# Both attentions of a two-layer kernel: value products of four heads at once, ScalarE's other work behind pairs of exponentials, and idle products in three places

## The chip, the cores and the metric

The kernel runs on one core of one Trainium2 chip. A core has TensorE (PE in the rows; PEld is its weight load), VectorE (DVE), ScalarE (ACT), GpSimd (POOL) and SyncE (SP), which issues DMAs. The metric is the device time of the core in microseconds; less is better. SBUF is the working memory, PSUM the matmuls' target, 8 banks of 2 KB per partition.

## The reference

Two layers act on x of 32 batches x 256 tokens x 128 features. Each layer: layer norm with a per-batch scale and shift, attention with 16 heads of 8 features, a residual with a per-batch gain; then layer norm again and a mixture of experts with a second gain.

```python
# layer 0                                     # layer 1
Qn, Kn = Q/|Q|, K/|K|   (per head)            q, kv = x @ Wq, x @ Wkv
attn = softmax(Qn Kn^T / sqrt(8))             attn = softmax(causal(q k^T / sqrt(8)))
out = (attn V) * gates;  x += ga * (out Wo + bo)   x += ga * ((attn V) Wo)
# then 4 experts, token-wise depth            # then top 2 of 8 experts
```

## The kernel before, in words

Every engine has a program written out by hand. Waits on semaphores (s["exp"], s["pv"], s["o"], ...) order them, and each engine runs its own list strictly in that order, so the order of the calls in the loops is the schedule. The phases are: modulation and first layer norm with the start of attention 0, attention 0 (function `dense` of each engine), experts 0, attention 1 (`causal`), rows sent to the experts, experts 1.

Both attentions loop over b = 0..31 (a batch of 256 tokens). A batch has 16 heads, taken two at a time in CH = 8 units u = 0..7. Four heads are a group j = u // 2, and NJ = 4. For each unit:

- TensorE `score(b, u)`: four matmuls (two key tiles x two heads) into the PSUM tile SP[u % 2] (L1873, L2118).
- ScalarE `exp(b, u)`: one exponential of SP[u % 2] into pt[u % 4] in SBUF (L750, L863); from the fifth unit on it waits for s["pv"], the product that frees the buffer.
- Attention 1 only, GpSimd `select(b, u)`: zeroes what the causal mask forbids in pt (L531).
- TensorE `values(b, u)` (L1892, L2138): the values of two heads, fp32, each in 32 columns of the array (tile_position (0, 32g)) and so in 32 partitions of OP. A column of ones beside the values gives the softmax's sum. It is issued two units late. OP has two halves (banks): half 0 holds groups j = 0, 1, half 1 holds j = 2, 3.

VectorE finishes a batch: `tail_t(b, i)` transposes half i of OP in 32 x 32 blocks (L1181, L1343) and raises s["o"]; `tail_n` (in attention 1 `tail_r`, `tail_n`, `tail_a`) divides by the sums and transposes to aT; TensorE's `tail_wo` is the output projection, into the free end of OP's half 1 (L1904, L2150); `tail_w` (L1199, L1366) takes it out and raises s["wr"]; then the gain, the residual `tail_x`, and the statistics of the next layer norm. tail_t(b, 0) closes VectorE's list of batch b, and tail_t(b, 1) stands at the head of the list of b + 1.

Between these, later batches are prepared and earlier ones finished. Attention 0: TensorE `project(b + 3)` (L1859), VectorE `take`, ScalarE `square`, VectorE `lengths` (L1155 and on), GpSimd `lengths` (a Newton iteration), VectorE `unit` (L1165), ScalarE `high` and VectorE `low` (L1174, the fp16 halves), then four transposing DMAs. A finished batch n goes through ScalarE `normal(n)` (needs GpSimd's `deviation`), TensorE `turn(n)` (L1915), ScalarE `enter(n)` (L770), TensorE `router(n)` (L1925), VectorE `extra(n)` (L1229) and `depth(n)`, GpSimd `low(n)`. Attention 1: twelve `fill`s per batch (L2092, L2097, L2101) form scores in M's two banks alternately, so that VectorE's `fill_max` (L1329) finds each row's maximum for the next batch; ScalarE `z2`, `enter`, `raw`, `high`, `z3`, `h3`, `row`; TensorE `enter`, `project` (L2076), `turn3`, `router`, `back`. `keep_warm` issues matmuls whose result nobody reads. From b = 15 on GpSimd also sends rows to the experts' buffers (L492).

## Time and profile before

| what | value |
|---|---|
| median of 3 runs | 1821.77 us (1817.3 to 1825.23) |
| the profiled execution | 1828.18 us, span 1826.0 us |
| TensorE busy | 1556.5 us (85%), 12803 matmuls |
| VectorE busy | 1284.0 us (70%) |
| ScalarE busy | 1188.8 us (65%) |
| GpSimd busy | 882.6 us (48%) |
| mean granted TensorE clock | 0.933 |
| attention 0 | from about 80 to 540 us |
| experts 0 | from about 540 to 770 us |
| attention 1 | from about 800 to 1430 us |
| experts 1 | from about 1500 us on |

The span cut into 40 equal slices of 45.65 us, busy share in tenths (9 is 90% or more), and the granted clock in tenths:

```profile
PE   5799999999967999779999999999999508989970
DVE  6566777777747888836767677675877536777768
ACT  3777788778756989635565665556555517888860
POOL 6254544545511333324444438747465563555554
PEclk9899999999988999969999999999999558999995
```

A row of a timeline gives the start and the time in microseconds, the engine, the line of the kernel, the operation, output and input tiles, their shapes, the count of merged instructions, and in brackets the idle time ahead of it with the engine and line that ended it. A row of a stretch gives its bounds and length, then the busy time and the instructions of TensorE, its weight load, VectorE, ScalarE and GpSimd, the granted TensorE clock as a share of full speed, the DMA engines' busy share and GB/s. Matmuls overlap, so the distance between two starts tells more than a row's length.

### The profile page before, as it was taken

The numbers are of one execution on the slowest core, as the hardware profiler recorded it, in microseconds if no ns is written. First come the engines' busy times: TensorE is split into PE (matmuls) and PEld (weight loads), VectorE is DVE, ScalarE is ACT, GpSimd is POOL, SyncE is SP. The second block draws the span as 40 slices with busy tenths as digits, with TensorE's granted clock in tenths as the row PEclk, the third lists the DMA queues.
The fourth block names the chain that finished last, engine by engine and source line by source line (L and its number), as shares of the span: only waits on it lengthen the run. The fifth ranks groups of instructions, "written<-read, shape, count | busy, mean of one in ns | idle before, by whom it ended". The sixth has DMA issues, their size and how long they took to land.

```text
span 1826.0 us, 39932 instructions
## 1 busy us (share of the span) xinstructions
PE 1556.5 (85%) x12803; PEld 796.7 (44%) x12803; DVE 1284.0 (70%) x3451; ACT 1188.8 (65%) x2134; POOL 882.6 (48%) x1677
## 2 busy tenths in 40 slices
PE   5799999999967999779999999999999508989970
PEld 3334444444433444324444444444444306777750
DVE  6566777777747888836767677675877536777768
ACT  3777788778756989635565665556555517888860
POOL 6254544545511333324444438747465563555554
PEclk9899999999988999969999999999999558999995
DMA  5221112221208930022211213312221323222228
GB/s 155 75 45 36 36 36 41 42 37 36 47 13 331 386 125 1 23 57 50 48 41 41 46 38 66 69 43 66 45 62 43 112 77 97 75 77 76 76 66 258
DMA packets 238478, 141.20 MB, mean 77 GB/s; under 512 B 184163, under 2 KB 210659, under 8 KB 237253
## 3 DMA queue, kind: packets, MB, share of 16 engines
q1 hardware_dynamic: 227072, 119.72, 24.4%
q0 software_dynamic: 8640, 17.97, 3.0%
q8 instruction: 108, 1.77, 0.4%
q10 hardware_dynamic: 2564, 0.97, 0.2%
q14 instruction: 94, 0.76, 0.1%
HBM read 37.67 MB, written 58.98 MB: 53 GB/s over the span
## 4 chain that ended last, share of the span: by engine, by line
PE 42%; DVE 12%; issue 6%; ACT 2%; DVEq 2%; POOL 2%; DMA 1%; POOLq 1%; SPq 0%; ACTq 0%; another core or an unknown queue 0%
PE OP L2138 8%; PE OP L2003 5%; PE M L2101 5%; PE SP L1983 4%; DVE mx L1329 4%; PE SP L2298 3%; PE SP L2118 2%; PE M L2076 2%; PE M L2097 2%; PE M L2092 2%; PE OP L2313 2%; DVE pt L1620 2%; POOL h_dram L492 1%; PE OP L2150 1%; PE M L1993 1%
## 5 line engine op out<-in xcount | busy, mean ns | idle before, releaser
L863 ACT ACTIVATE pt<-SP 128x768 f32<-128x768 f32 x256 | 207.1, 809 | 250.4 <-PE SP L2118 236.4
L1329 DVE TENSOR_REDUCE mx<-M 128x2 f32<-128x512 f32 (+1 forms) x384 | 258.0, 683 | 104.5 <-PE M L2101 94.6
L531 POOL TENSOR_SCALAR_AFFINE_SELECT pt<-pt 128x256 f32<-128x256 f32 x512 | 198.6, 412 | 262.8 <-ACT pt L863 260.9
L750 ACT ACTIVATE pt<-SP 128x1024 f32<-128x1024 f32 x256 | 255.2, 1019 | 72.1 <-PE SP L1873 72.0
L562 POOL DMA_INDIRECT y_dram<-hT,dest x142 | 140.2, 987 | 134.2 <-DVE hT L1626 112.0
L964 ACT ACTIVATE pt<-SP,b 128x256 f16<-128x256 f32 x284 | 138.2, 487 | 81.8 <-PE SP L2298 81.2
L1892 PE MATMUL OP<-pt,vs 128*32 128x256 f32 x1408 | 186.5, 387 | 0.0
L492 POOL DMA_INDIRECT h_dram<-hT,slot x128 | 130.7, 1021 | 58.8 <-issue 31.7
L2138 PE MATMUL OP<-pt,vs 128*32 128x128 f32 (+1 forms) x1408 | 151.0, 338 | 4.7 <-POOL pt L531 4.7
L1620 DVE TENSOR_TENSOR pt<-vs,pt 128x256 f16<-128x256 f32 x284 | 115.7, 428 | 49.8 <-ACT vs L965 25.0
L656 POOL TENSOR_TENSOR st<-st,ksT 128x512 f32<-128x512 f32 x48 | 72.0, 1500 | 153.1 <-DVE ksT L1751 153.0
L965 ACT ACTIVATE vs<-SP,b 128x256 f32<-128x256 f32 x284 | 139.5, 491 | 0.0
L2298 PE MATMUL SP<-ksT,shared 128*128 128x256 f16 x852 | 129.6, 276 | 10.0 <-DVE ksT L1595 10.0
L2313 PE MATMUL OP<-shared,pt 128*128 x1704 | 130.6, 219 | 0.4 <-issue 0.2
L1734 DVE TENSOR_TENSOR pt<-vs,pt 128x512 f16<-128x512 f32 x128 | 104.7, 830 | 26.6 <-ACT vs L982 25.2
L577 POOL TENSOR_TENSOR nt<-rn 128x64 f32<-128x64 f32 x96 | 34.2, 357 | 166.3 <-DVE rn L1018 156.7
L2313 PEld LDWEIGHTS OP<-shared,pt 128*128 128x128 f16 x1704 | 107.1, 98 | 12.5 <-issue 0.8
L980 ACT ACTIVATE pt<-SP,b 128x512 f16<-128x512 f32 x128 | 88.0, 688 | 26.5 <-PE SP L1983 23.0
L2101 PE MATMUL M<-ksT,shared 24*128 24x128 f16 (+1 forms) x704 | 105.2, 250 | 0.0
L1873 PE MATMUL SP<-shared 32*128 32x256 f16 x1024 | 100.3, 274 | 3.6 <-ACT pt L750 3.5
L1892 PEld LDWEIGHTS OP<-pt,vs 128*32 128x32 f32 x1408 | 66.6, 109 | 72.0 <-ACT pt L750 19.6
L2138 PEld LDWEIGHTS OP<-pt,vs 128*32 128x32 f32 x1408 | 67.0, 110 | 69.5 <-issue 22.7
(325 smaller groups left out, 3344.9 us busy)
## 6 DMA issues: line engine op xcount, KB each, us to landing
h_dram<-shared SPq DMA_DIRECT2D x8, 4488.0 KB, 33.5
hT<-h_dram SPq DMA_DIRECT2D x71, 132.0 KB
rows<-g_dram SPq DMA_DIRECT2D x4, 2048.0 KB, 7.1
pt<-y_dram SPq DMA_DIRECT2D x32, 256.0 KB, 3.7
x_sb<-in_x SPq DMA_DIRECT2D x8, 512.0 KB, 8.8
pt<-in_w SPq DMA_DIRECT2D x4, 1024.0 KB
out<-x_sb SPq DMA_DIRECT2D x16, 256.0 KB, 3.0
shared<-st SPq DMA_TRANSPOSE x144, 2.4
```

Of the source, the lines that this page charges most:

```text
L492: pool.indirect_dma_start(out=h_dram, out_offset=bass.IndirectOffsetOnAxis(ap=slot[:, TT * b0 + t, k:k + 1], axis=0), in_=hrow[:, q % 2, t ...
L531: last = pool.affine_select(out=diag, in_=diag, compare_op=ALU.is_ge, fill=0.0, base=0, pattern=[[0, 2], [1, P]], channel_multiplier=-1)
L562: pool.indirect_dma_start(out=y_dram, out_offset=bass.IndirectOffsetOnAxis(ap=dest[:, g % XB, r:r + 1], axis=0), in_=ys[:, g % XB, r, :], ...
L750: act.activation(pt[:, u % 4], SP[u % 2][:], ACT.Exp, scale=SCALE).then_inc(s["exp"], 1)
L863: act.activation(pt[:, u % 4, :, 0:384], SP[u % 2][:, :, 0:384], ACT.Exp, scale=SCALE).then_inc(s["exp"], 1)
L1329: dve.tensor_reduce(to, M[:, k % 2, :].rearrange("p (j k) -> p j k", j=4 if k < 4 else 2), AX.X, ALU.max).then_inc(s["mred"], 1)
L1620: dve.tensor_tensor(hid1[:, g % 2, f, 1, :], relu[:, f, 0:BLK], hid1[:, g % 2, f, 0, :], ALU.subtract).then_inc(k["lo"], 1)
L1892: last = pe.matmul(OP[32 * g:32 * g + 32, j // 2, c:c + T], vsd[b % 3][:, k, HG * j + g, :], pt[:, u % 4, i, k * T:k * T + T], start=(k == ...
L2101: last = pe.matmul(v[:, n, :], qs3[b % 3][32 * g:32 * g + 3 * DH, j, q0:q0 + P], ks3[b % 3][32 * g:32 * g + 3 * DH, j, 0:kn], start=False, ...
L2138: last = pe.matmul(OP[32 * g:32 * g + 32, j // 2, c + q0:c + T], vs3[b % 3][:, k, HG * j + g, :], pt[:, u % 4, i, k * T:k * T + T - q0], s ...
L2298: last = pe.matmul(bank[f][:, 0:BLK], w16[1][:, 0, u, bass.ds(e * (F1 * P) + f * P, P)], hg[:, g % 2, v, :], start=(n == 0), stop=(n == 2))
L2313: last = pe.matmul(to[:, r, :], hid1[:, g % 2, f, v, r * P:(r + 1) * P], w16[1][:, 1, u, bass.ds(e * (F1 * P) + f * P, P)], start=False, s ...
```

## The change

- `values(b, j)` replaces `values(b, u)`: four heads (16 matmul records) in one go, interleaved over the four column groups, at every odd u, when both exponentials (in attention 1 both selects) are there. It raises s["pv"] by 2. At u = 1 it is group 3 of the batch before.
- ScalarE in attention 0: `normal`, `high`, `square` and `enter` stand behind pairs of exponentials; `normal` and `enter` handle batch b - 4, not b - 3.
- TensorE in attention 0: the two halves of `project` are at u = 2 and u = 4 (before both at u = 1), `turn(b - 4)` at u = 6, `router(b - 5)` at u = 2 of the next batch. GpSimd's `low`, VectorE's `extra` and `depth` handle b - 5. `extra` moves behind `tail_n`.
- Idle products: attention 0, four after score(b, 0) into OP's half 0, which wait for s["o"] >= 2b - 1 (tail_t(b - 1, 0)), and three after the turn at u = 6 into half 1, which wait for s["wr"] >= b. Attention 1, one before the third, fifth and sixth fill, where no `keep_warm` stands.
- Attention 1: the product comes before the fills of u = 1 and after the first fill of u = 3; TensorE's `enter(b + 3)` is behind score 7 and ahead of the product, `turn3(b - 5)` behind the product of u = 7. On VectorE the tail steps come one to three column maxima earlier.

```diff
@@ ScalarE, dense
     for b in range(B):
         exp(b, 0)
         exp(b, 1)
+        if b >= 4:
+            normal(b - 4)
         exp(b, 2)
         if b == 0:
             sigmoid()
+        exp(b, 3)
         if b + 2 < B:
             high(b + 2)
-        exp(b, 3)
         exp(b, 4)
+        exp(b, 5)
         if b + 3 < B:
             square(b + 3)
-        if b >= 3:
-            normal(b - 3)
-        exp(b, 5)
         exp(b, 6)
-        if b >= 3:
-            enter(b - 3)
         exp(b, 7)
+        if b >= 4:
+            enter(b - 4)
         if b < CHUNKS:
             weight_high(0, b)
-    for n in range(B - 3, B):
+    for n in range(B - 4, B):
         normal(n)
         enter(n)
...
@@ VectorE, dense
     static_gate()
     dve.drain()
     for b in range(B):
-        if b >= 4:
-            extra(b - 4)
         if b == 1:
             dve.wait_ge(gate_in, 16 * HG)
             dve.wait_ge(row_in, 16)
         if b:
             tail_t(b - 1, 1)
             tail_n(b - 1)
+        if b >= 5:
+            extra(b - 5)
         if b + 2 < B:
             unit(b + 2)
         if b + 3 < B:
...
@@ VectorE, causal
                 fill_max(b + 1, k)
                 if k in (7, 11):
                     max_row(b + 1, k // 11)
+            if b and k == 0:
+                tail_t(b - 1, 1)
             if b and k == 2:
-                tail_t(b - 1, 1)
-            if b and k == 4:
                 tail_r(b - 1)
-            if b and k in (5, 6):
-                tail_n(b - 1, k - 5)
-            if b and k == 7:
+            if b and k in (3, 4):
+                tail_n(b - 1, k - 3)
+            if b and k == 5:
                 tail_a(b - 1)
             if b and k == 10:
                 tail_w(b - 1)
...
@@ TensorE, dense: values
                                  start=True, stop=True, tile_position=(r0, 0))
         last.then_inc(s["score"], 1)
-    def values(b, u):
-        if u == 0:
+    def values(b, j):
+        if j == 0:
             pe.wait_ge(s["vs"], b + 1)
-        pe.wait_ge(s["exp"], CH * b + u + 1)
-        if b and u % 4 == 0:
-            pe.wait_ge(s["o"], 2 * b + u // 4 - 1)
-            if u:
+        pe.wait_ge(s["exp"], CH * b + 2 * j + 2)
+        if b and j % 2 == 0:
+            pe.wait_ge(s["o"], 2 * b + j // 2 - 1)
+            if j:
                 pe.wait_ge(s["wr"], b)
-        j = u // 2
+        c = (j % 2) * T
         for k in range(TT):
-            for i in range(2):
-                g = 2 * (u % 2) + i
-                c = (j % 2) * T
+            for g in range(HG):
                 last = pe.matmul(OP[32 * g:32 * g + 32, j // 2, c:c + T],
                                  vsd[b % 3][:, k, HG * j + g, :],
-                                 pt[:, u % 4, i, k * T:k * T + T],
+                                 pt[:, 2 * (j % 2) + g // 2, g % 2, k * T:k * T + T],
                                  start=(k == 0), stop=(k == TT - 1),
                                  skip_group_check=True, tile_position=(0, 32 * g))
-        last.then_inc(s["pv"], 1)
+        last.then_inc(s["pv"], 2)
     def tail_wo(b):
...
@@ TensorE, dense: idle
             last = pe.matmul(M[:, 1, t * nx:(t + 1) * nx], hcur[:, n % 2, t * P:(t + 1) * P], wx[1][:],
                              start=True, stop=True)
         last.then_inc(s["lg"], 1)
+    def idle(half, n):
+        for _ in range(n):
+            pe.matmul(OP[:, half, :].rearrange("p (n q) -> p n q", n=4), identb[:],
+                      maskQ[:].unsqueeze(1).to_broadcast([P, 4, P]), start=True, stop=True, skip_group_check=True)
     for n in range(B + 2):
         gates(n)
...
@@ TensorE, dense: the loop
             score(b, u)
             if b == 0 and u == 2:
                 pe.wait_ge(gl_in, 1)
-            if CH * b + u >= 2:
-                values((CH * b + u - 2) // CH, (u - 2) % CH)
-            if u == 1 and b + 3 < B:
-                for t in range(TT):
-                    project(b + 3, t)
+            if u % 2 and CH * b + u >= 3:
+                values((CH * b + u - 3) // CH, (u - 3) % CH // 2)
+            if u == 0 and b:
+                pe.wait_ge(s["o"], 2 * b - 1)
+                idle(0, 4)
+            if u == 2 and b >= 5:
+                router(b - 5)
+            if u in (2, 4) and b + 3 < B:
+                project(b + 3, u // 2 - 1)
             if u == 4 and b:
                 tail_wo(b - 1)
-            if u == 5 and b >= 3:
-                turn(b - 3)
-            if u == 7 and b >= 3:
-                router(b - 3)
-    values(B - 1, CH - 2)
-    values(B - 1, CH - 1)
+            if u == 6 and b >= 4:
+                turn(b - 4)
+                pe.wait_ge(s["wr"], b)
+                idle(1, 3)
+    values(B - 1, NJ - 1)
     tail_wo(B - 1)
-    for n in range(B - 3, B):
+    router(B - 5)
+    for n in range(B - 4, B):
         turn(n)
         router(n)
...
@@ TensorE, causal: the loop (values there is as above, with s["sel"])
         done = 0
         for u in range(CH):
             score(b, u)
-            if FILLS[u] and b + 1 < B:
-                fill(b + 1, done)
-                done += 1
-            if CH * b + u >= 2:
-                values((CH * b + u - 2) // CH, (u - 2) % CH)
             if u == 0 and b + 2 < B:
                 project(b + 2, 0)
                 project(b + 2, 1)
             if u == 4 and b:
                 tail_wo(b - 1)
-            for _ in range(FILLS[u] - 1):
-                if b + 1 < B:
+            if u == 7 and b + 3 < B:
+                enter(b + 3)
+            for n in range(max(FILLS[u], 1)):
+                if n == (u == 3) and u % 2 and CH * b + u >= 3:
+                    values((CH * b + u - 3) // CH, (u - 3) % CH // 2)
+                if FILLS[u] and b + 1 < B:
                     if done == 2 and b in WARM:
                         keep_warm(b, u + 1, WARM[b])
+                    elif done in (2, 4, 5) and b:
+                        pe.wait_ge(s["o"], 2 * b - 1)
+                        idle(0, 1)
                     fill(b + 1, done)
                     done += 1
             if u == 5 and b >= 6:
                 router(b - 6)
                 back(b - 6)
-            if u == 6:
-                if b + 3 < B:
-                    enter(b + 3)
-                if b >= 5:
-                    turn3(b - 5)
+            if u == 7 and b >= 5:
+                turn3(b - 5)
             if u == 7 and b - 1 in CHOSEN:
                 positions(CHOSEN.index(b - 1))
-    values(B - 1, CH - 2)
-    values(B - 1, CH - 1)
+    values(B - 1, NJ - 1)
     tail_wo(B - 1)
     for n in range(B - 5, B + 1):
         if n < B:
```

## Rows read from the trace of the kernel before

**Rows 1.** busy time and granted clock: first attention, second attention, after a stand

```profile
172.00:514.00 342.00, 333.12 (x2710) 142.53 (x2708) 247.20 (x734) 271.32 (x370) 164.15 (x484) 1.00 0.20 38
898.00:1070.00 172.00, 164.22 (x1436) 80.01 (x1434) 122.98 (x293) 103.88 (x178) 72.41 (x172) 1.00 0.22 43
131.40:135.00 3.60, 3.60 (x20) 1.00 (x16) 0.97 (x3) 3.35 (x5) 2.36 (x8) 0.53 0.49 99
```

**Rows 2.** timeline, ScalarE: last exponentials of batches 0, 8, 28, 31

```profile
90.25 1.95 ACT L750 ACTIVATE pt<-SP 128x1024 f32<-128x1024 f32 x2
...
208.06 1.03 ACT L750 ACTIVATE pt<-SP 128x1024 f32<-128x1024 f32 x1
...
486.28 1.03 ACT L750 ACTIVATE pt<-SP 128x1024 f32<-128x1024 f32 x1
...
524.50 1.03 ACT L750 ACTIVATE pt<-SP 128x1024 f32<-128x1024 f32 x1
```

**Rows 3.** timeline, TensorE, one batch of the first attention

```profile
305.71 0.66 PE L1925 MATMUL M<-wx,hcur 128*128 128x68 f32 x4
306.30 0.39 PE L1873 MATMUL SP<-shared 32*128 32x256 f16 x4
...
307.94 1.06 PE L1892 MATMUL OP<-pt,vs 128*32 128x256 f32 x8
308.92 1.56 PE L1859 MATMUL M<-wqkv,hT 128*128 128x384 f32 x4
310.41 0.39 PE L1873 MATMUL SP<-shared 32*128 32x256 f16 x4
...
314.34 0.71 PE L1904 MATMUL OP<-wo,aT 128*128 128x128 f32 x4
```

**Rows 4.** timeline, TensorE, two products in a row

```profile
525.45 1.18 PE L1892 MATMUL OP<-pt,vs 128*32 128x256 f32 x16
```

**Rows 5.** timeline, VectorE, two batches of the first attention

```profile
307.36 0.70 DVE L1181 STREAM_TRANSPOSE oT<-OP 128x512 f32<-128x512 f32 x1
...
309.04 0.72 DVE L1181 STREAM_TRANSPOSE oT<-OP 128x512 f32<-128x512 f32 x1 [0.80 <-PE OP L1892]
...
312.23 1.01 DVE L1147 TENSOR_TENSOR shared<-M,bqkv 128x384 f32<-128x384 f32 x2
315.09 0.43 DVE L1199 TENSOR_TENSOR ao<-OP,bo 128x256 f32<-128x256 f32 x1 [1.84 <-PE OP L1904]
...
317.15 0.68 DVE L1155 TENSOR_REDUCE n<-sq 128x64 f32<-128x512 f32 x1
...
321.95 0.71 DVE L1181 STREAM_TRANSPOSE oT<-OP 128x512 f32<-128x512 f32 x1
...
329.02 0.42 DVE L1199 TENSOR_TENSOR ao<-OP,bo 128x256 f32<-128x256 f32 x1 [2.09 <-PE OP L1904]
...
331.78 0.68 DVE L1155 TENSOR_REDUCE n<-sq 128x64 f32<-128x512 f32 x1
...
334.81 0.70 DVE L1181 STREAM_TRANSPOSE oT<-OP 128x512 f32<-128x512 f32 x1
```

**Rows 6.** timeline, TensorE, one batch of the second attention

```profile
994.61 1.56 PE L2076 MATMUL M<-wqkv,hT 128*128 128x384 f32 x4
...
999.94 0.84 PE L2138 MATMUL OP<-pt,vs 128*32 128x256 f32 x8
1000.72 0.28 PE L2097 MATMUL M<-maskQ,identb 128*128 128x256 bf16 x1
...
1013.81 1.56 PE L2076 MATMUL M<-wqkv,hT 128*128 128x384 f32 x4
```

**Rows 7.** timeline, ScalarE, end of a batch of the second attention

```profile
1009.94 0.81 ACT L863 ACTIVATE pt<-SP 128x768 f32<-128x768 f32 x1 [1.02 <-PE SP L2118]
...
1012.10 0.81 ACT L863 ACTIVATE pt<-SP 128x768 f32<-128x768 f32 x1 [0.86 <-PE SP L2118]
1012.81 0.56 ACT L833 ACTIVATE hT<-M,modT 128x256 f32<-128x256 f32 x1
```

More of the change, by code:

```diff
@@ L638, in dense @@
                         place_v(b + 2)
-                    if b >= 4:
-                        low(b - 4)
+                    if b >= 5:
+                        low(b - 5)
                     if b + 3 < B:
@@ L644, in dense @@
                         weight_low(b - 1)
-                low(B - 4)
                 deviation(B // 2 - 1)
-                for n in range(B - 3, B):
+                for n in range(B - 5, B):
                     low(n)
@@ L1295, in dense @@
                         tail_x(b - 1)
-                    if b >= 4:
-                        depth(b - 4)
+                    if b >= 5:
+                        depth(b - 5)
                     if b:
@@ L1311, in dense @@
                 variance(B // 2 - 1)
-                for n in range(B - 4, B):
+                for n in range(B - 5, B):
                     extra(n)
@@ L2121, in score, with values @@
                     last.then_inc(s["score"], 1)
-                def values(b, u):
-                    if u == 0:
+                def values(b, j):
+                    if j == 0:
                         pe.wait_ge(s["vs"], b + 1)
-                    pe.wait_ge(s["sel"], CH * b + u + 1)
-                    if b and u % 4 == 0:
-                        pe.wait_ge(s["o"], 2 * b + u // 4 - 1)
-                        if u:
+                    pe.wait_ge(s["sel"], CH * b + 2 * j + 2)
+                    if b and j % 2 == 0:
+                        pe.wait_ge(s["o"], 2 * b + j // 2 - 1)
+                        if j:
                             pe.wait_ge(s["wr"], b)
-                    j = u // 2
+                    c = (j % 2) * T
                     for k in range(TT):
                         q0 = P if k else 0
-                        for i in range(2):
-                            g = 2 * (u % 2) + i
-                            c = (j % 2) * T
+                        for g in range(HG):
                             last = pe.matmul(OP[32 * g:32 * g + 32, j // 2, c + q0:c + T],
                                              vs3[b % 3][:, k, HG * j + g, :],
-                                             pt[:, u % 4, i, k * T:k * T + T - q0],
+                                             pt[:, 2 * (j % 2) + g // 2, g % 2, k * T:k * T + T - q0],
                                              start=(k == 0), stop=(k == TT - 1),
                                              skip_group_check=True, tile_position=(0, 32 * g))
-                    last.then_inc(s["pv"], 1)
+                    last.then_inc(s["pv"], 2)
                 def tail_wo(b):
@@ L2193, in back, with idle @@
                     last.then_inc(s["back"], 1)
+                def idle(half, n):
+                    for _ in range(n):
+                        pe.matmul(OP[:, half, :].rearrange("p (n q) -> p n q", n=4), identb[:],
+                                  maskQ[:].unsqueeze(1).to_broadcast([P, 4, P]), start=True, stop=True, skip_group_check=True)
                 def keep_warm(b, u, n):
```

9 lines of the change are left out of this document (4 added, 5 removed).

## The prediction

> **What bounds the kernel now.** The page first: by its slices TensorE is 90% busy or more through both attentions, VectorE and ScalarE between 50 and 80%. So I took each attention by its own stretch. In the first one TensorE is busy 333.12 of 342 us, ScalarE 271, VectorE 247; in the second 164.22 of 172 us, VectorE 123, ScalarE 104 [rows 1]. The reader is to see that TensorE's order of work sets the pace of both, and that neither other engine is full. The exponentials give the length of a batch. In the first attention b = 0 ends its exponentials at 91.2 (the second of the pair in the row), b = 8 at 208.06, b = 28 at 486.28, b = 31 at 524.50: 14.6 us a batch for the first eight, 13.91 for the next twenty, 12.7 for the last three [rows 2]. In the second, projections repeat at 994.61 and 1013.81: 19.20 us a batch [rows 6].
>
> The third view is the order of time on TensorE and VectorE within one batch, because a gain on TensorE is kept only if no circle through another engine is as long as the batch. That is where most of this forecast is decided.
>
> **The products.** A values product of two heads (8 matmul records; every instruction is two passes) holds TensorE for 0.98 us (307.94 to 308.92) [rows 3]; the second attention's for 0.78 (999.94 to 1000.72) [rows 6]. The change sends four heads' instructions side by side. The trace before has a case: at the end of the first attention two products follow each other with no scores between, and all 16 records take 1.18 us from first start to last end [rows 4], against 1.06 for 8 [rows 3]. So four column groups stream at once. I take 1.00 for a four-head product and 0.80 in the second attention; the bounds are 0.98 and 1.96 (no overlap at all). Removed per batch: 8 x 0.98 = 7.84, added 4 x 1.00: -3.84 us. Second: 8 x 0.78 - 4 x 0.80 = -3.04.
>
> **The idle products.** Seven of 512 bf16 columns in a batch of the first attention, three in the second (two where a longer warming stands). I price one at a step of a values product, four steps in 0.98 us, so 0.22; bounds 0 (TensorE would have waited) and 0.25. That is 1.54 and 0.66 us.
>
> TensorE's work in the first attention so falls from 13.7 to about 11.4 us a batch. It does not set the pace any more, and here is what does.
>
> **First attention: the circle through VectorE.** Call t0 VectorE's transpose of OP's first half (end of its batch's list), t1 the transpose of the second half (head of the next list). In the new order TensorE, after score 0, waits for t0 before four idle products into that half; then score 1, and only then values(b-1, 3), which t1 needs. t1 stands ahead of the whole list that ends in the next t0. So t0 -> idle -> score 1 -> values -> t1 -> list -> t0 is closed once per batch, whatever the phases. Before, t0 was asked for only by values(b, 0), behind the product that t1 needs, and t1 followed t0 without waiting for it.
> - t0 to t1, new: 0.71 for t0 and 0.05 to release; idle 4 x 0.22 = 0.88; score 0.33 (of 307.94 to 314.34, 6.40, four products and one pair of projections leave 0.33 for each of three scores); product start to t1 as before, 309.04 - 307.94 = 1.10, plus 0.02. Sum 3.09. Before: 1.68 (307.36 to 309.04) [rows 3, 5].
> - t1 to the bias step on OP (L1199), which waits for the output projection: before, 6.05 (309.04 to 315.09), with 1.84 us of it idle, TensorE being late. New TensorE path from the product's start: 1.00 + score 0.33 + router 0.59 (305.71 to 306.30) + projection 0.75 (half of 308.92 to 310.41) + 0.33 + 1.00 + 0.33 + 0.75, then 0.75 from output projection to L1199 (314.34 to 315.09) = 5.83, less the 1.12 before t1: 4.7. VectorE's own work there is 4.20 (309.04 to the end of the row at 312.23) plus 0.26 for the router's bias, which moves in: 4.5. So 4.7.
> - L1199 to the sum of squares: 2.06 in one batch, 2.76 in the next (315.09 to 317.15, 329.02 to 331.78). From there to t0: 4.80 with the variance step, 3.03 without. Means 2.41 and 3.92 [rows 5]. All VectorE's own; the change leaves them.
> - Circle: 3.09 + 4.7 + 2.41 + 3.92 = 14.1 us, against 13.91 now. A floor, with VectorE never waiting for the output projection, is 13.9.
>
> So 3.8 us less on TensorE gain nothing per steady batch: TensorE will stand 2 to 3 us at the first idle product. Twenty batches cost 20 x 0.2 = +4. Batches 1 to 4 have no router or depth step on VectorE (I estimate 13.0), 5 to 8 go at 14.1: 108.4 for what took 116.9 [rows 2], -8.5, as the normalisation comes a batch later and no one waits for it. The last three lose projections and lengths: some 34 for 38.2, -4. One more batch is normalised and routed behind the loop: +1. Together -7 (bounds -23, with the floor and no cost at the ends, and +5).
>
> **ScalarE's and GpSimd's moved work** (normal, high, square, enter in pairs of exponentials; low and extra a batch later) I cost at nothing: ScalarE is busy 271 of 342 us [rows 1]. `square` behind one more exponential still lies inside L1199 to L1155; if that cover goes, it costs 0.1 to 0.5 us in every batch. No DMA is added, and SP's queue keeps its order.
>
> **The clock.** A stand of 2 to 3 us is new here. At 131.4, right behind a stand of TensorE for a normalised tile, the granted clock was 0.53, so nearly all at 1.2 of 2.4 GHz, although the engine was busy for the whole 3.6 us [rows 1]. A stretch of that kind behind the new stand falls on score 1 and its product, on the circle, and costs up to 0.47 x 3.6 = 1.7 us. The idle products work against it. I take a fifth of the full price of 28 batches: +10, bounds 0 and +48. First attention: -7 + 10 = +3.
>
> **Second attention.** Here VectorE has room: TensorE had 164 of 172 busy, VectorE 123. TensorE's sum goes 19.20 - 3.04 + 0.66 = 16.8. Two waits eat part. First, `enter` (TensorE) now follows score 7, and project waits for ScalarE's enter: from score 6, 0.38 to the exponential at 1009.94, then to ScalarE's enter 2.87 less its wait of 0.86 = 2.01, and 0.56 for enter itself: 2.95 [rows 7]. TensorE has between them four short score/enter steps, a product and turn3, some 2.35. So +0.6. Second, twelve column maxima alternate with fills over two banks, and VectorE's list between them hardly shortens: I give 0.4 (bounds 0 and 1.2). GpSimd's sends take a microsecond each beside its selects in a third of the batches, inside the same 0.4. Period 17.85, or -1.35 in 31 batches: -42 (bounds -73, all of TensorE's saving, and -17).
>
> **A rule on the change.** What the trace shows is that TensorE's evacuation by VectorE, not the array, closes the first attention's circle [rows 5]. The Trainium skill, page TensorEngine Tiling (Array Packing), section PSUM Bottleneck, says tiling speeds up TensorE and not the emptying of PSUM, which may become the bottleneck. By that rule, the trace agrees for the first attention. Its figures for column tiles belong to rival F.
>
> **Sum.** The profiled execution took 1828.18 us: 1828.2 - 42 + 3 = 1789. The runs' median, 1821.77, lies 6.4 below it: **1783**.
>
> **Rivals.**
> - A, the forecast, 1783 (1755 to 1805): chance 0.55.
> - B, the first attention keeps TensorE's saving: the circle is shorter than I add up, because VectorE's steps run faster when its neighbours are spread out. For: steps vary (2.06 and 2.76). Against: every term is a start-to-start time without waits. At 12.6 us a batch, 28 x 1.5 less, 1741. 0.12.
> - C, the second attention keeps all of its own: 17.85 to 16.85, 1783 - 31 = 1752. For: the fill stretch shows few waits. Against: project behind enter. 0.13.
> - D, slower, by one mechanism: the clock. If every batch of both attentions meets one stretch like that of rows 1 on its path, 1.7 us each, 59 batches cost 100 instead of the 10 I took: 1873. It decides from about 0.8 us a batch, where the gain is gone. Against: the second attention leaves no long stand. 0.06.
> - E, the change doesn't do what it says: only two column groups at a time. Then each four-head product is 0.96 (0.76) longer, two of them on the first circle: +1.9 x 24 = +46, and the second keeps 19.86, 62 more than forecast: 1891. Against: the x16 row. 0.04.
> - F, four groups overlap, but not fully: a product goes a quarter of the way to 1.96 (1.56), 0.24 and 0.19 more than I took. Two lie on the first circle: 0.48 x 24 = +12; four in the second: 0.76 x 31 = +24; 1819. For: the 1.18 of rows 4 is 0.12 over a single product. Against: so small a part. 0.10. The Trainium skill, page TensorE: Matmul & The Clock Gate, section Part 3: Packing small matmuls, gives 2.38x for three column tiles, not 3x; an estimate by its rate (3/2.38) would put a product near 1.25.
>
> A measurement of this kernel tells a change from none at about 0.5%, 9 us. Faster: A, B, C and what of F lies under 1812, 0.85; same, the rest of F and the top of A, 0.07; slower, D and E with a little of A, 0.08. The range 1740 to 1812 takes in B and C and leaves out D, E and most of F.
>
> **What would show it.** Right: sixteen records of a product in about 1.05 us in both attentions; VectorE's t0 to t0 at 14 us, its wait before L1199 near nothing, and a wait of TensorE for VectorE's L1181 of 2 to 3 us at score 0's idle products; projections in the second attention 17.5 to 18.2 us apart, preceded by a wait for ScalarE's L833. Wrong: a first-attention batch under 13.5 us (a term of the circle is too long), products of 1.5 us or more, second-attention batches over 18.8, or a granted clock below 0.9 in either.

## The result and the profile after

The change makes the kernel slower: 1910.51 us median (1889.77 to 1920.75, 4 runs) against 1823.5 (1817.3 to 1829.41, the three runs listed above and a fourth). The ratio is 1.044, with a 95% interval of 1.0345 to 1.0534. Ratios here and below are of the fast runs alone, so this one leaves out the run of 1920.75, and a ratio can differ a little from that of the medians. The forecast was 1783, so even the sign was wrong.

Stage by stage, from first to last exponential for an attention, one line each of the profile's busy times. Columns as in [rows 1]: stretch, its length, busy time and instructions of TensorE, its weight loads, VectorE, ScalarE, GpSimd, then the granted clock of TensorE, DMA share, GB/s. Before:

```profile
80.10:524.50 444.40, 428.60 (x3462) 181.28 (x3464) 310.23 (x898) 349.59 (x472) 206.79 (x605) 0.99 0.19 37
810.40:1428.30 617.90, 583.91 (x5071) 282.95 (x5075) 437.38 (x1058) 354.64 (x598) 338.44 (x687) 0.99 0.23 50
1513.10:1767.00 253.90, 232.13 (x2869) 193.13 (x2867) 189.72 (x664) 212.52 (x563) 134.62 (x137) 0.99 0.24 72
```

After, the same three stages, and then the stretches that answer to [rows 1]:

```profile
78.20:566.70 488.50, 407.06 (x3654) 167.87 (x3658) 301.18 (x892) 346.40 (x465) 191.47 (x604) 0.86 0.18 34
855.00:1508.10 653.10, 606.57 (x5148) 276.48 (x5152) 432.31 (x1058) 353.68 (x598) 336.66 (x684) 0.80 0.22 47
1595.10:1829.90 234.80, 229.47 (x2869) 193.34 (x2867) 184.77 (x666) 213.88 (x565) 138.43 (x137) 0.99 0.26 77
...
172.00:514.00 342.00, 281.31 (x2528) 118.08 (x2520) 218.01 (x656) 238.79 (x326) 138.56 (x442) 0.87 0.18 35
898.00:1070.00 172.00, 163.06 (x1378) 73.42 (x1376) 111.86 (x259) 92.63 (x155) 68.53 (x163) 0.79 0.21 43
...
384.00:387.40 3.40, 2.03 (x26) 0.64 (x24) 2.56 (x13) 3.35 (x5) 1.10 (x4) 1.00 0.69 77
387.90:397.70 9.80, 9.57 (x54) 3.37 (x54) 3.56 (x9) 4.54 (x7) 3.54 (x10) 0.50 0.14 27
398.00:401.30 3.30, 3.30 (x36) 1.81 (x33) 2.16 (x5) 2.54 (x5) 0.00 (x0) 1.00 0.00 0
```

The first attention is 44 us longer and the second 35. The reader is to see the column of the clock: 0.99 fell to 0.86 and 0.80. It takes two levels only, 1.00 (2.4 GHz) and 0.50 (1.2 GHz), as in the last three rows, so the share of a stage at half clock is twice what is missing from 1: 28% of the first attention and 40% of the second. Summed from the clock's records that is 140 us (it was 7) and 257 us (it was 14). The profiled execution after is the shortest of its four runs, and its last stage, which the change doesn't touch, is 19 us shorter than before's; without that it would have been near the median. On that stage, see the end.

**One batch at each clock, first attention.** VectorE after, the steps of [rows 5] (VectorE's line numbers are one lower than before's). One batch from 452.98 at full clock, and one from 387.38 that meets the stretch at half clock:

```profile
387.38 0.70 DVE L1180 STREAM_TRANSPOSE oT<-OP 128x512 f32<-128x512 f32 x1
392.50 0.72 DVE L1180 STREAM_TRANSPOSE oT<-OP 128x512 f32<-128x512 f32 x1 [4.42 <-PE OP L1889]
...
399.52 0.41 DVE L1198 TENSOR_TENSOR ao<-OP,bo 128x256 f32<-128x256 f32 x1
...
401.57 0.68 DVE L1154 TENSOR_REDUCE n<-sq 128x64 f32<-128x512 f32 x1
...
406.14 0.71 DVE L1180 STREAM_TRANSPOSE oT<-OP 128x512 f32<-128x512 f32 x1
...
452.98 0.70 DVE L1180 STREAM_TRANSPOSE oT<-OP 128x512 f32<-128x512 f32 x1
456.16 0.72 DVE L1180 STREAM_TRANSPOSE oT<-OP 128x512 f32<-128x512 f32 x1 [2.48 <-PE OP L1889]
...
460.71 0.41 DVE L1198 TENSOR_TENSOR ao<-OP,bo 128x256 f32<-128x256 f32 x1
463.26 0.69 DVE L1154 TENSOR_REDUCE n<-sq 128x64 f32<-128x512 f32 x1 [0.42 <-ACT sq L730]
467.84 0.71 DVE L1180 STREAM_TRANSPOSE oT<-OP 128x512 f32<-128x512 f32 x1
```

| step of the circle | forecast | at full clock | with half clock |
|---|---|---|---|
| t0 to t1 | 3.09 | 3.18 | 5.12 |
| t1 to bias step | 4.7 | 4.55 | 7.02 |
| to sum of squares | 2.41 (mean) | 2.55 | 2.05 |
| to next t0 | 3.92 (mean) | 4.58 (with variance) | 4.57 |
| batch | 14.1 | 14.86 | 18.76 |

The same two batches on TensorE; L1929 are the idle products:

```profile
388.13 1.89 PE L1929 MATMUL OP<-maskQ,identb 128*128 128x512 bf16 x4 [2.10 <-DVE oT L1180]
389.96 0.61 PE L1872 MATMUL SP<-shared 32*128 32x256 f16 x4
390.49 1.94 PE L1889 MATMUL OP<-pt,vs 128*32 128x256 f32 x16
...
406.91 0.39 PE L1929 MATMUL OP<-maskQ,identb 128*128 128x512 bf16 x1 [3.15 <-DVE oT L1180]
...
453.73 1.04 PE L1929 MATMUL OP<-maskQ,identb 128*128 128x512 bf16 x4 [2.31 <-DVE oT L1180]
454.70 0.39 PE L1872 MATMUL SP<-shared 32*128 32x256 f16 x4
455.02 1.07 PE L1889 MATMUL OP<-pt,shared 128*32 128x256 f32 x16
```

TensorE stands 2.10 us for t0; behind it its products take about twice as long, and four idle products (0.97 us at full clock, start to start 453.73 to 454.70) take 1.83. At full clock a four-head product takes 1.01 us (455.02 to the next start at 456.03), against 0.98 for two heads [rows 3]; forecast 1.00. The page of the whole run shows the circle (after `|`: busy time, mean ns of one, then the idle time ahead and what ended it):

```profile
L1929 PE MATMUL OP<-maskQ,identb 128*128 128x512 bf16 x208 | 63.3, 428 | 76.8 <-DVE oT L1180 76.8
L1180 DVE STREAM_TRANSPOSE oT<-OP 128x512 f32<-128x512 f32 x64 | 45.5, 711 | 109.1 <-PE OP L1889 108.9
```

Each engine waits for the other, 76.8 and 108.9 us. The last exponential of b = 31, at 524.50 before [rows 2], now starts at 566.71. The two products in a row of [rows 4] are now one four-head product.

**Second attention.** TensorE after, from one pair of projections to the next but one, as in [rows 6]:

```profile
1052.73 1.78 PE L2083 MATMUL M<-wqkv,hT 128*128 128x384 f32 x4
...
1058.20 0.39 PE L2099 MATMUL M<-maskQ,identb 128*128 128x512 bf16 x1 [0.48 <-DVE mx L1328]
...
1066.06 0.86 PE L2143 MATMUL OP<-pt,vs 128*32 128x256 f32 x16
...
1070.51 1.89 PE L2083 MATMUL M<-wqkv,hT 128*128 128x384 f32 x4 [0.39 <-ACT hT L832]
...
1076.09 0.39 PE L2099 MATMUL M<-maskQ,identb 128*128 128x512 bf16 x1 [0.48 <-DVE mx L1328]
...
1083.24 0.28 PE L2104 MATMUL M<-maskQ,identb 128*128 128x256 bf16 x1 [0.25 <-DVE mx L1328]
...
1083.94 1.51 PE L2143 MATMUL OP<-pt,hT 128*32 128x256 f32 x16
1085.38 1.02 PE L2182 MATMUL M<-wx,hcur 128*128 128x8 f32 x4
...
1090.33 2.93 PE L2083 MATMUL M<-wqkv,hT 128*128 128x384 f32 x4
```

The first batch takes 17.78 us (forecast 17.85), with 0.86 for a product; the second, with the same work, 19.82, since from 1083.94 on products take 1.51. The five such periods with less than 1 us at half clock took 17.78 to 18.24, one of them 19.58; most others took 19 to 25. No long stand comes before the fall at 1083.9: only waits of 0.2 to 0.5 us for VectorE's maxima, with short matmuls between them. The wait for ScalarE's enter [rows 7] ahead of the projection is 0.39.

### The profile page after: what moved, and what is told of

The parts are those of the page before. It is cut to its first block, busy times and chain, and to the rows that moved or that the text cites. A ratio compares the mean times of both kernels' runs of the same rounds, so it can differ in the third digit from the quotient of the medians.

```text
span 1887.7 us, 40519 instructions
## 1 busy us (share of the span) xinstructions
PE 1555.9 (82%) x13097; PEld 778.2 (41%) x13097; DVE 1266.1 (67%) x3451; ACT 1188.3 (63%) x2134; POOL 873.1 (46%) x1677
## 4 chain that ended last, share of the span: by engine, by line
PE 43%; DVE 13%; issue 3%; POOL 3%; DVEq 2%; ACT 1%; DMA 1%; POOLq 1%; SPq 1%; ACTq 0%
PE OP L2143 5%; PE OP L2322 5%; DVE mx L1328 5%; PE SP L2307 5%; PE OP L2010 4%; PE SP L1990 4%; PE M L2108 4%; PE M L2104 2%; PE M L2083 2%; PE SP L2125 2%; POOL h_dram L492 2%; DVE oT L1342 1%; PE OP L2155 1%; PE M L2182 1%; PE M L2000 1%
## 5 line engine op out<-in xcount | busy, mean ns | idle before, releaser
L562 POOL DMA_INDIRECT y_dram<-hT,dest x142 | 144.0, 1014 | 110.5 <-DVE hT L1625 88.6
L1929 PE MATMUL OP<-maskQ,identb 128*128 128x512 bf16 x208 | 63.3, 428 | 76.8 <-DVE oT L1180 76.8
L1180 DVE STREAM_TRANSPOSE oT<-OP 128x512 f32<-128x512 f32 x64 | 45.5, 711 | 109.1 <-PE OP L1889 108.9
L2108 PE MATMUL M<-ksT,shared 24*128 24x128 f16 (+1 forms) x704 | 117.5, 271 | 0.0
L1872 PE MATMUL SP<-shared 32*128 32x256 f16 x1024 | 110.3, 298 | 3.8 <-ACT pt L749 3.2
L1889 PE MATMUL OP<-pt,vs 128*32 128x256 f32 x1408 | 113.1, 447 | 0.1
L2143 PE MATMUL OP<-pt,vs 128*32 128x256 f32 (+1 forms) x1408 | 96.4, 403 | 8.6 <-issue 4.5
```

What stands on the lines that cost most here:

```text
L562: pool.indirect_dma_start(out=y_dram, out_offset=bass.IndirectOffsetOnAxis(ap=dest[:, g % XB, r:r + 1], axis=0), in_=ys[:, g % XB, r, :], ...
L2108: last = pe.matmul(v[:, n, :], qs3[b % 3][32 * g:32 * g + 3 * DH, j, q0:q0 + P], ks3[b % 3][32 * g:32 * g + 3 * DH, j, 0:kn], start=False, ...
L2143: last = pe.matmul(OP[32 * g:32 * g + 32, j // 2, c + q0:c + T], vs3[b % 3][:, k, HG * j + g, :], pt[:, 2 * (j % 2) + g // 2, g % 2, k * T ...
```

## Experiments

Each is compared with the kernel before, timed beside it; that one took 1810.67 us beside e1 to e4, 1836.87 beside e5 to e8, 1843.85 beside e9 to e11 and 1828.65 beside e12, so only the ratios compare kernels across these groups. "The stage" is from first to last exponential, time at half clock is summed from the clock's records within it. A batch is called undisturbed when it meets no stretch at half clock. Parts of the change are applied to the kernel before, if nothing else is said; only e7, e11 and e12 have both parts.

| run | kernel, us | ratio (95%) | att. 0: stage / half clock | att. 1: stage / half clock |
|---|---|---|---|---|
| before (profile above) | | | 444.4 / 7 | 617.9 / 14 |
| the change | 1910.51 | 1.044 (1.0345 to 1.0534) | 488.5 / 140 | 653.1 / 257 |
| e1_att0_only | 1854.39 | 1.0224 (1.0169 to 1.0279) | 481.8 / 126 | 634.1 / 57 |
| e2_att1_only | 1863.51 | 1.029 (1.0235 to 1.0345) | 450.9 / 21 | 659.2 / 280 |
| e3_att1_idle3 | 1819.36 | 1.0031 (0.9989 to 1.0073) | 444.4 / 7 | 625.1 / 130 |
| e4_att0_open | 1793.31 | 0.99 (0.9852 to 0.9949) | 419.6 / 68 | 626.8 / 39 |
| e5_att1_u4 | 1845.02 | 1.0037 (1.0009 to 1.0066) | 445.4 / 7 | 631.8 / 75 |
| e6_att0_shared_bank | 1782.5 | 0.9716 (0.9661 to 0.9772) | 388.5 / 7 | 626.7 / 39 |
| e7_both_mended | 1790.22 | 0.9741 (0.9693 to 0.9789) | 389.9 / 14 | 631.6 / 75 |
| e8_att1_no_idle | 1949.88 | 1.0631 (1.0572 to 1.069) | 441.5 / 0 | 736.8 / 525 |
| e9_att0_warm_stand | 1845.62 | 1.0004 (0.9979 to 1.0029) | 443.6 / 7 | 636.4 / 63 |
| e10_att0_no_warm | 1784.02 | 0.968 (0.9641 to 0.9718) | 388.7 / 24 | 626.8 / 40 |
| e11_both_idle2 | 1779.94 | 0.967 (0.9625 to 0.9715) | 390.5 / 14 | 613.9 / 78 |
| e12_change_warmed | 1826.59 | 0.9979 (0.9959 to 0.9999) | 444.6 / 10 | 613.6 / 81 |

**The two parts apart.** e1 takes the first attention's hunks of the diff and leaves the second attention as before; e2 the reverse.

> The change in the first attention alone; the second is as before. Theory (the circle t0, idle, score 1, values, t1, VectorE's list lets TensorE stand about 2 to 3 us a batch, and the clock falls behind it): the first attention takes 40 to 50 us longer than before, mean granted clock of the whole run about 0.88, total about 1865 us (1845 to 1885). Rival (the loss sits in the second attention and the first gains what TensorE lost): 1790 or less with the clock at 0.93.

> The change in the second attention alone. Theory (in the fills' stretch VectorE sets the pace, TensorE has two products fewer there, and its clock falls): second attention 30 to 40 us longer, clock about 0.87, total about 1857 us (1835 to 1880). Rival (new waits in the order of enter and project at full clock): the same total with the clock at 0.93. Second rival (the first attention's loss alone): 1780.

Both are slower by themselves, +2.2% and +2.9%, and each own stage is within 7 us of the change's. Each stage's excess over before is near what was expected: 37 us for 40 to 50, and 41 for 30 to 40. So the loss is in both parts; their product, 1.0224 x 1.029 = 1.052, is a little more than the whole change's 1.044.

**More idle work in the second attention.** e3:

```
-                                    idle(0, 1)
+                                    idle(0, 3)
```

> As the second attention's change alone, with three idle products instead of one ahead of the third, fifth and sixth fill. Theory (clock): they lie where TensorE waits for VectorE, the clock comes back to 0.92 or more over the run, batches take about 18.2 us, total 1780 to 1800 us. Rival (TensorE's own work sets the pace): six more idle products of 0.22 us in 31 batches add 41 us to the run without them.

Adding 1.3 us of useless products a batch made the stage 34 us shorter than e2's: 659.2 to 625.1. The direction is that of "clock", the size is not: the kernel's clock came back to 0.90 and its time to 1819.36, where 0.92 and 1780 to 1800 were expected, and 130 us stayed at half clock. The other direction, e8, takes the change's idle products out:

```
-                                elif done in (2, 4, 5) and b:
-                                    pe.wait_ge(s["o"], 2 * b - 1)
-                                    idle(0, 1)
```

> Second attention's part alone as in e2_att1_only (1863.5 us) with its three idle products left out. Theory 'clock': TensorE stands more at the stretch ahead of the fills, more time at half clock than the 280 us of e2_att1_only or as much, and the kernel takes 1860 to 1900 us. Rival 'extra work': the idle products (three of 0.22 us in 31 batches, 20 us) and their wait for VectorE's transpose are what made the second attention slower; then the kernel takes 1840 to 1845 us.

Its second attention:

```profile
807.10:1543.90 736.80, 690.78 (x5064) 307.13 (x5068) 434.91 (x1058) 355.81 (x598) 335.66 (x684) 0.64 0.20 42
```

TensorE has 20 us less work than in e2 and the stage takes 78 more, at a clock of 0.64. The rival "extra work" is out, and "clock" holds, by more than its range (1949.88 us, +6.3% on the kernel before beside it). Of the 17 stretches at half clock left in e3, 13 began 1.9 to 2.9 us behind the output projection's start, in the stretch u = 4, where the change took a product away; the others lie at the stage's ends but for one. (The expectation of e5 says "all".) In the change itself 8 of 21 begin there, most others 14 to 21 us behind it, in the next batch. e5 fills that place too:

```
 def idle_half(n):    # 128x256 into OP[:, 0, T:2 * T]
...
+                                elif done in (9, 10) and b:
+                                    idle_half(4)
```

> Second attention's part alone as in e3_att1_idle3 (idle(0, 3) ahead of fills 2, 4 and 5), and in addition four small idle products (128x256 each, about 0.12 us at full clock) ahead of fills 9 and 10, written to the free columns of the half that the next pair of heads' product uses. In e3_att1_idle3 the half-clock stretches of the second attention (130 us of 625) all begin in this stretch of the batch, where the moved product had been. Theory 'clock': the falls go, half-clock time in the second attention falls below 40 us, its batches are 18.2 to 18.5 us, the stage takes 585 to 600 us and the kernel 1780 to 1795 us. Rival 'order': what costs is the new order on VectorE and the extra work of the idle products, not the clock; then the stage takes 625 us or more, the kernel 1820 to 1830 us, whatever the clock is.

Half true. The steady falls went: none begins in u = 4, and four are left between the stage's ends. But 75 us at half clock is above the 40 expected, and the stage of 631.8 is no shorter than e3's and lies where the rival put it. The undisturbed batch is 18.9 us, nearly all of it TensorE's own work (132.31 of 140 us busy at full clock from 940 on), against 19.2 before the change. The warm products cost 2.9 us a batch (9 x 0.22 + 8 x 0.11), which is nearly the 3.04 that the new products save. e11 takes part of them back, on top of e7:

```
-                                    idle(0, 3)
+                                    idle(0, 2)
...
-                                    idle_half(4)
+                                    idle_half(3)
```

> e7_both_mended with fewer idle products in the second attention: two ahead of fills 2, 4 and 5 in place of three, and three small ones ahead of fills 9 and 10 in place of four: 0.9 us a batch less. In e5_att1_u4 and e7_both_mended the undisturbed batch takes 18.9 us, which is TensorE's own sum. Theory: TensorE sets the batch there, so each batch that meets no fall is 0.8 to 0.9 us shorter (18.0 to 18.1), and with falls in no more than a third of the batches (up to 110 us at half clock) the stage takes 600 to 620 us against 631.6: the kernel is 10 to 28 us faster than e7_both_mended and the fastest of all, 0.960 to 0.969 of the kernel before. Rival: the work that is left out is what keeps the clock, and comes back as time at half clock (over 130 us), stage 625 us or more, no gain: 0.974 or more.

Second attention in e11: its clock is that of e5 with 0.9 us less work a batch (undisturbed batches 18.25 us).

```profile
758.90:1372.80 613.90, 566.99 (x5416) 269.00 (x5419) 438.25 (x1058) 351.22 (x598) 336.74 (x684) 0.94 0.24 50
```

The theory holds for the stage, 613.9 against e7's 631.6. For the kernel it isn't shown: 0.967 against 0.9741, measured in different groups, with intervals that overlap. Its warm work is that of e3, 2.0 us a batch, but spread over the stretches that are thin: 78 us at half clock against 130, and 11 us less. Of the 78, 63 lie in three stretches: one of 22.3 at the stage's start and two of 20.5. They are why a batch that is 0.9 us shorter than before the change makes the stage only 4 us shorter than the 617.9.

**The first attention, circle or clock.** e9 leaves the circle as the change has it and fills the stand ahead of it:

```
                         if u == 0 and b:
+                            pe.wait_ge(s["exp"], CH * b)
+                            for _ in range(8):
+                                pe.matmul(SP[1][:, 0, :]...)        # 128x512, as in idle
                             pe.wait_ge(s["o"], 2 * b - 1)
                             idle(0, 4)
```

> First attention's part alone, with its circle of batches left as the change has it (wait for VectorE's transpose, idle(0, 4), scores, values(b-1, 3)), and eight more warm products (0.22 us each, 1.75 us a batch) into the scores' second bank in the stand of 2 to 3.7 us ahead of that wait, where TensorE does nothing in e1_att0_only. It tells the two causes apart. If the circle alone makes the first attention what it is, and the clock falls are only extra: falls go (half-clock time there below 30 us against 126), a batch takes 14.3 to 14.6 us as the undisturbed ones do, the stage 452 to 462 us against 481.8, and the kernel 1.007 to 1.014 of the kernel before. Rival: the falls do not follow from that stand: half-clock time stays over 90 us, the stage over 475 us, the kernel 1.02 or more. Third: the warm products come in the circle's way, each batch longer by up to 1.7 us: stage over 490 us at full clock.

VectorE in e9, one even and one odd batch:

```profile
318.74 0.71 DVE L1180 STREAM_TRANSPOSE oT<-OP 128x512 f32<-128x512 f32 x1
321.93 0.72 DVE L1180 STREAM_TRANSPOSE oT<-OP 128x512 f32<-128x512 f32 x1 [2.49 <-PE OP L1889]
...
331.95 0.70 DVE L1180 STREAM_TRANSPOSE oT<-OP 128x512 f32<-128x512 f32 x1
335.13 0.72 DVE L1180 STREAM_TRANSPOSE oT<-OP 128x512 f32<-128x512 f32 x1 [2.49 <-PE OP L1889]
...
346.80 0.71 DVE L1180 STREAM_TRANSPOSE oT<-OP 128x512 f32<-128x512 f32 x1
```

Batches of 13.21 and 14.85 us, t0 to t1 3.2 in both: the circle of the forecast, 14.0 by the mean of these two and 14.2 by that of the 22 steady ones from 170 us on. The stage is 443.6 us, as before (444.4), at a clock of 0.99. That is less than the 452 to 462 I expected, and so is the kernel's ratio, 1.0004 for 1.007 to 1.014; the circle by itself costs nothing against before. So the circle eats the whole of TensorE's saving and the clock alone makes the loss in this attention. TensorE in e9 still waits for t0 behind the warm products, which shows that they don't hold it up:

```profile
316.01 1.90 PE L1953 MATMUL SP<-maskQ,identb 128*128 128x512 bf16 x8 [0.20 <-ACT pt L749]
319.50 1.04 PE L1929 MATMUL OP<-maskQ,identb 128*128 128x512 bf16 x4 [1.59 <-DVE oT L1180]
```

**Opening the circle.** e4 moves the wait and its idle products behind values(b-1, 3):

```
-                        if u == 0 and b:
+                        if u == 1 and b:
                             pe.wait_ge(s["o"], 2 * b - 1)
                             idle(0, 4)
```

> As the first attention's change alone, but the wait for t0 and the four idle products stand behind values(b-1, 3) at u = 1, so that t1 no longer hangs on t0. Theory (circle): TensorE's stand goes, batches take 12 to 13 us, the clock is 0.93 over the run, total about 1785 us (1765 to 1805). Rival (TensorE has too little to do for its clock wherever it waits): clock 0.88 or less, total above 1840.

t1 now follows right behind t0 (one row of 1.30 us holds both, at 304.72) in place of 3.18 later, undisturbed batches take 12.1 and 13.3, and the stage is 25 us shorter than before, though 68 us of it are at half clock. The time, 1793.31, is within what was expected; the clock of the run, 0.909, is not the 0.93. e6 drops the wait:

```
-                        if u == 1 and b:
-                            pe.wait_ge(s["o"], 2 * b - 1)
-                            idle(0, 4)
...
+                        if u == 2 and b:          # ahead of score(b, 2), which uses the same bank
+                            pe.wait_ge(s["exp"], CH * b + 1)
+                            for _ in range(4):
+                                pe.matmul(SP[0][:, 0, :]...)
```

> First attention's part alone. As e4_att0_open, but TensorE does not wait for VectorE's transpose at all for its idle products: four of them go into the scores' bank ahead of score(b, 2), where the bank is free because the exponential before has been read out. Theory: the wait inside the circle of batches was what made the first attention slow, and with the falls that begin at a stand of TensorE gone too a batch takes 12.0 to 12.6 us where e4_att0_open had 13.3: stage 385 to 405 us instead of 419.6, half-clock time below 50 us, kernel 1770 to 1785 us. Rival: the idle products' place doesn't matter, since a stand behind values(b-1, 3) stays as long as before (VectorE's copy of the weighted values is what it waits for): stage 415 to 425 us and the kernel 1790 to 1800 us.

VectorE in e6:

```profile
315.73 1.31 DVE L1180 STREAM_TRANSPOSE oT<-OP 128x512 f32<-128x512 f32 x2
...
327.06 1.30 DVE L1180 STREAM_TRANSPOSE oT<-OP 128x512 f32<-128x512 f32 x2
...
340.41 1.30 DVE L1180 STREAM_TRANSPOSE oT<-OP 128x512 f32<-128x512 f32 x2
```

Both transposes run as one row, batches take 11.33 and 13.35 us by turns, 12.3 by the mean, and the stage is 388.5: 56 us shorter than before. The rival (the stand stays whatever the idle products' place) is out. e10 leaves the four products ahead of score(b, 2) out of e6:

> e6_att0_shared_bank without its four warm products ahead of score(b, 2): they cost 0.9 us of TensorE a batch and are there only for the clock. Theory 'clock': with 0.9 us less work of 12.4 the falls come back: half-clock time in the first attention 60 us or more against 6.8, stage 400 to 415 us against 388.5, and slower than e6_att0_shared_bank by 10 to 25 us. Rival: with the wait out of the circle TensorE is busy enough without them: stage 380 to 389 us, and the kernel as fast as e6_att0_shared_bank or up to 8 us faster.

That expectation failed. The falls do not come back in number (24 us at half clock), the stage is the same, and the ratios, 0.968 and 0.9716, can't be told apart. With the wait gone TensorE is busy 329 of 389 us and keeps its clock nearly throughout, where the change had it busy 407 of 488 and lost it: in both it does nothing for about a sixth of the time. The difference is in how that time is cut. Between 172 and 514 us the change has 21 waits for t0 that sum to 58.6 us, the longest 4.1. In e10, between 172 and 460, waits for ScalarE and VectorE sum to 44 us in 75 pieces, most under 1.3, the longest 2.1. e4 lies between: it is busier than e10 (374 of 420 us), but has 20 waits for t0 that sum to 31.4 us, and 68 us at half clock. So in this attention the runs point to the length of the single stands, and not to the share of time in which TensorE had work. e9 agrees, where filling the stand was enough. No run keeps the change's stand and varies its length alone.

**Both together.** e7 is e6 and e5 in one kernel, e12 the whole change with its order untouched and warm products alone added (e9's in the first attention, e11's in the second).

> The two mended halves together: first attention as in e6_att0_shared_bank, second as in e5_att1_u4. If stages add as they did between e1_att0_only, e2_att1_only and the full change, the time is that of e5_att1_u4 plus that of e6_att0_shared_bank less the kernel before: 1740 to 1775 us. Rival: the clock falls in the one attention depend on what the other did (the unchanged second attention of e1_att0_only had 57 us at half clock against 14), so the sum is missed by 20 us or more.

> The whole change with its order left as it is and warm products alone added: in the first attention the eight of e9_att0_warm_stand, in the second those of e11_both_idle2 (two ahead of fills 2, 4 and 5, three small ones ahead of fills 9 and 10). TensorE gets 1.75 us more work a batch in the first and about 1.4 us in the second. Theory: the whole loss of the change (87 us) was clock, so time at half clock in the two attentions falls from 397 us to below 130 us, first attention 443 to 448 us, second 612 to 622 us, the kernel 0.985 to 0.999 of the kernel before. Rival: the two attentions' falls depend on each other or on the chip, and the kernel stays above 1.005.

e7 took 1790.22. The parts add: e5's time plus e6's less the kernel before beside them is 1845.02 + 1782.5 - 1836.87 = 1790.65. The 1740 to 1775 expected was too low because it counted on a second attention of 585 to 600 us, which e5 did not have (631.8). e12's two attentions:

```profile
80.40:525.00 444.60, 407.88 (x3902) 175.08 (x3906) 307.45 (x892) 342.11 (x466) 193.61 (x603) 0.99 0.18 37
813.70:1427.30 613.60, 568.21 (x5414) 269.57 (x5417) 437.41 (x1058) 350.90 (x598) 335.68 (x684) 0.93 0.24 50
```

Nothing was taken out of the change; 1.75 us of useless work a batch of the first attention and 1.3 us of the second were added. Time at half clock in the two attentions went from 397 us to 91, and 1.044 became 0.9979, with the stages at 444.6 and 613.6 us for 444.4 and 617.9 before. Work that only keeps TensorE busy can't shorten a circle or a wait, so this shows the cause: the loss of 87 us was clock. The best version measured is e11_both_idle2, 0.967 (0.9625 to 0.9715), not to be told apart from e10.

## Why the prediction was wrong, point by point

- **The products and the idle products**: right. 1.01 and 0.78 us (1066.06 to the next start at 1066.84) for 1.00 and 0.80; an idle product 0.24 (four in 0.97) for 0.22. Rivals E and F are out. The Trainium skill, page TensorE: Matmul & The Clock Gate, section Part 3: Packing small matmuls, gives 2.38x for three column tiles. From two groups to four this trace shows no such loss, 1.01 us against 0.98; one group alone was not run.
- **The circle of the first attention**: right in mechanism and nearly in size. Every term is within 0.25 us of the undisturbed batches, also `square` behind one more exponential: VectorE waits 0.4 to 0.5 us for it in 9 of the batches between 172 and 514, inside the 0.1 to 0.5 that I gave if the cover went. TensorE's stand for t0, forecast at 2 to 3 us, was 2.8 by the mean (58.6 us in 21). The -7 us for the stage came out as -1 (e9). Rival B is out for this order; e6 shows that the saving was there once the wait was not in the circle.
- **The clock in the first attention: the failed step.** "I take a fifth of the full price of 28 batches: +10, bounds 0 and +48." It measured +45 (488.5 against e9's 443.6), nearly the upper bound. Two things were too low. I discounted the number: 21 stretches at half clock lie in the 32 batches. And I priced each at 3.6 us of half clock, where they last 3.4 to 13.7, with up to 3.9 us lost in a batch (18.76 against 14.86). Nothing in the trace of before supported a fifth: the one row that showed a stand (131.4, clock 0.53 [rows 1]) showed the full price.
- **The clock in the second attention: a term that was left out.** I gave it no cost since "the second attention leaves no long stand". The batch of 17.85 came nearly true where hardly a fall met it (17.78 to 18.24 in four periods, 19.58 in one); with the falls the stage was +35 instead of -42. A long stand is not needed. Thinner work (3.04 us less a batch, a product moved out of u = 4) with waits of 0.2 to 0.5 us was enough, and e8 shows the slope: 20 us less work, 245 us more at half clock, 78 us longer. The Trainium skill, page TensorE: Matmul & The Clock Gate, section A second HAM failure mode: psum-queue depth-cycling, tells of another kernel whose TensorE pauses briefly and often between groups of matmuls and swings between its clocks. These rows agree, with waits of 0.2 to 0.5 us and a clock of 0.79. I had not weighed it, and rival D deserved more than the least chance but one.
- **Rival D** is what happened: 1873 by its price of 1.7 us in every batch. I gave it 0.06. Its "against", that the second attention leaves no long stand, was true and did not help. My last sign of being wrong, a clock below 0.9 in either attention, is what the rows of the stretches show (0.87 and 0.79).
- **The range** left out exactly the mechanism whose cost I could bound least. With its upper bound in both attentions, +48 and +53, the sum is 1783 - 10 + 101 = 1874, still under the 1910 measured, since the falls last longer than the one in [rows 1] and the second attention lost more than +53 against its forecast: +77 (653.1 against 617.9 - 42).

## What to carry to other kernels

When a change makes TensorE's work shorter but another engine or a circle of waits sets the period, the time saved turns into gaps, and the gaps can cost the clock: look where in a batch TensorE is thinnest after the change, and price a fall there in full, with the work behind it doubled, until a run shows otherwise. Products that only keep the engine busy should not wait for anything that is not ready anyway: with four such products behind VectorE's transpose a steady batch took 14.2 us (e9), with four in the scores' own bank 12.3 (e6), and with none the same (e10). Their place counts as well as their number (130 against 78 us at half clock for the same 2.0 us a batch, e3 and e11).

## What the runs showed that I had not expected

- A stage that no kernel here changes, the routed experts, took 252 to 255 us in the profiles of before and of e5 to e12, and 234 to 235 in those of the change and of e1 to e4, in each set whatever the kernel was. The page's line for the same step in before and after:

```profile
L1620 DVE TENSOR_TENSOR pt<-vs,pt 128x256 f16<-128x256 f32 x284 | 115.7, 428 | 49.8 <-ACT vs L965 25.0
```

```profile
L1619 DVE TENSOR_TENSOR pt<-vs,pt 128x256 f16<-128x256 f32 x284 | 112.6, 425 | 35.9 <-ACT vs L964 34.7
```

Part of VectorE's idle time ahead of this step ends with nothing that the profile shows: 24.3 us in before, 0.9 after. The kernel before, too, ran at 1810.67 beside e1 to e4 and at 1828.65 to 1843.85 beside the others. e1 to e4 ran on one chip, e5 to e12 on three others. So it belongs to where or when a kernel runs, not to the change; what it is stays open. It is why kernels are compared above by ratios to runs made alongside. The attentions don't show it: the first one, unchanged in before, e3 and e5, took 444.4, 444.4 and 445.4.
- Unchanged code lost clock after changed code: the second attention as before took 617.9 us with 14 at half clock in before, 634.1 with 57 in e1, 626.7 with 39 in e6, 636.4 with 63 in e9. About half of it is one stretch at the stage's start in e1, e6 and e9 (29, 22 and 29 us, against 4 before), but e5, whose first attention is that of before, has 22 us there too. So the changed code ahead is not shown to be the cause, and the cause stays open; it sets a limit of some 9 to 19 us on how far one stage's saving can be read from the kernel's time.
